# Four transposes of layer 3 go behind the next unit's first score in TensorE's queue

## The chip, the cores and the metric

One core of one Trainium2 chip runs the whole program in one launch. The metric is the device time in microseconds; the kernel before took 2738.4 us (median of 3 runs, 2736.6 to 2738.7). The profile shows one more execution, of 2738.3 us, with a span of 2737.0 us.

## The reference

Thirty-two sequences of 256 tokens with 256 features pass through four layers. Layer 0 is a conditioned MLP with a norm over the whole sequence, layer 1 is attention with 16 heads, an additive bias and a mask, and an MLP, layer 2 is a stencil over the 256 x 256 grid, layer 3 is causal attention with 16 heads and an MLP:

```
h  = layernorm(x, gamma1, beta1)
attn = softmax(causal(h Wq @ (h Wk)^T / 4)) @ (h Wv)
x1 = x + attn @ Wo + bo
h2 = layernorm(x1, gamma2, beta2)              # m4 (statistics), m4_norm, t4, t4_out
ff = gelu(h2 @ W1 + b1) @ W2 + b2              # w3, w3_out, w3_gelu, w4
x2 = x1 + ff
return x + gate * (x2 - x)
```

All of it is computed. The change touches only when the transposes of `h2` (before gamma2 and beta2) stand in TensorE's queue.

## The kernel before

The program is software-pipelined over a clock of ticks. A sequence b starts every 64 ticks; its layer 3 starts 160 ticks later than its layer 1. Each attention layer is cut into 8 units of two heads, one unit every 4 ticks, so layer 1 of a sequence and layer 3 of another take turns. Between the units' pieces stand the dense pieces of the layers (projections, MLPs, stencil, norms). The table `P` gives each piece its tick within its sequence or unit; `OWN` overrides it for the first two and the last two sequences. Each engine walks through the ticks and issues the pieces that are due, in a fixed order within a tick; nothing else sets the order. Engines wait for each other by semaphores, and each queue is in order: what stands behind a waiting instruction waits too.

On TensorE a tick issues first the attention pieces (score0, score1, flip0, flip1, pv0, pv1), then the dense ones; t4 and w3 are the last but one and two of the list. In the middle sequences the ticks 50 to 57 of layer 3 of sequence b hold, on TensorE: 50 score0 of unit 5 of layer 1 of sequence b + 3, 51 the flips of unit 3, 52 score1 of unit 5 and the pv pieces of unit 2, 53 t4, 54 score0 of unit 6, 55 the flips of unit 4 and w3 step 0, 56 score1 of unit 6 and pv of unit 3, 57 w3 step 1. Ticks 59 and 61 have w3 steps 2 and 3.

The pieces that the prediction follows:

- score0 (L1191): one matmul of the stacked queries Qs and keys Ks, 96 rows deep, into PSUM bank bS[0]. It waits for the stack (d_st) and for VectorE to have read the bank's previous score (v_bias, L786).
- The stack: for every second unit SP issues nine DMAs, three of Qs (L407) and six of Ks (L411), from SBUF to SBUF, into one of two buffers. SP's queue also has the bias loads BT (L396), which wait for VectorE's bias piece of four units earlier, and the loads of x and the mask.
- flip0, flip1 (L1199): four transposes each of the probabilities PB, after ScalarE's exp (L990). ScalarE copies them out as PH (L996).
- m4_norm (ScalarE, L1005): writes the normalised rows TC. t4 (TensorE, `turn`, L1163): four transposes of TC into bank bT_. t4_out (ScalarE, L1011): TN from that bank, with gamma2 and beta2. In ScalarE's queue: flip copies of unit 3, m4_norm, exp1 of unit 4, t4_out, exp0 of unit 5, flip copies of unit 4, w3_out step 0.
- w3 step g (TensorE, `widen`, L1171, eight matmuls of TN into bank bT_), w3_out step g (ScalarE, L1011, BB from the bank). One bank serves all four steps, so step g + 1 waits for w3_out of step g.

Of the kernel before, what the change touches and what calls it, by code (L numbers as in the profile page):

```python
# [42 lines left out]
def begin(layer, b):  # L43
# [32 lines left out]
}  # L76

LATE = {
# [44 lines left out]
        "s_b": 88, "s_r": 88, "s_rp": 90, "s_re": 95, "s_ha": 95, "s_w": 96, "s_ab": 97, "s_row": 98, "s_mm": 100,  # L123
# [3 lines left out]
    },  # L127
    1: {
        "score0_1": 1, "score1_1": 3, "bias0_1": 3, "exp0_1": 6, "flip0_1": 11, "flip1_1": 11, "high0_1": 12,
# [1311 lines left out]
```

## Time and profile before

| | us |
|---|---|
| median of 3 runs | 2738.4 |
| profiled execution, time | 2738.3 |
| its span | 2737.0 |
| TensorE matmul busy | 2599.0 |
| ScalarE busy | 2338.8 |
| VectorE busy | 2221.9 |
| GpSimd busy | 1674.0 |

A row of the time line gives the start, the length, the engine (PE is TensorE's matmuls, PEld its weight loads, DVE VectorE, ACT ScalarE, SPq SyncE's queue of DMA issues), the line, the operation, output and inputs by the program's names, the shape, how many instructions are merged (x4), and in brackets how long the engine sat idle before and what ended that. A matmul's length is its latency; the next one may start before it ends.

### The profile page before, as it was taken

Reading aid. Unit: us, or ns where it says so; the run is one execution under the profiler, and the core shown is the slowest. Engines: PE = TensorE matmul, PEld = TensorE weight load, DVE = VectorE, ACT = ScalarE, POOL = GpSimd, SP = SyncE. Lnnn points to the kernel's source line nnn. Section 1 sums busy time; section 2 is a strip of 40 time slices with the busy share of each in tenths; the row PEclk is TensorE's granted clock in tenths of the full one; section 3 lists DMA queues with packets and bytes.
Section 4 is the critical chain, followed back from the end, with each engine's and each line's share of the span. In section 5 each row is a group of like instructions: output and inputs, shape, how many; then the busy total and the mean of one; then the engine's idle time right before and its main releaser. Section 6 shows DMA issues by size and latency. Waiting matters only on the chain.

```text
span 2737.0 us, 62626 instructions
## 1 busy us (share of the span) xinstructions
PE 2599.0 (95%) x20072; PEld 2214.0 (81%) x20072; DVE 2221.9 (81%) x7925; ACT 2338.8 (85%) x5285; POOL 1674.0 (61%) x1742
## 2 busy tenths in 40 slices
PE   8888999999999999999999999999999999999987
PEld 7766888888888888888888888888888888888776
DVE  5668888888888888888888888888888888888753
ACT  1567899999999999998999989999998998999865
POOL 2666666766667675666666566666666666765431
PEclk8988999999999999999999999999999999999999
DMA  6433343333333333333333333343333333333211
GB/s 230 130 96 102 91 118 108 116 102 113 96 103 115 109 114 103 110 98 101 114 112 112 103 108 101 98 119 108 113 97 114 101 100 116 109 105 102 63 31 29
DMA packets 176549, 287.96 MB, mean 105 GB/s; under 512 B 45856, under 2 KB 99104, under 8 KB 175840
## 3 DMA queue, kind: packets, MB, share of 16 engines
q1 hardware_dynamic: 176224, 283.97, 35.2%
q8 instruction: 162, 2.65, 0.4%
q14 instruction: 163, 1.34, 0.2%
HBM read 174.64 MB, written 8.45 MB: 67 GB/s over the span
## 4 chain that ended last, share of the span: by engine, by line
PE 71%; ACT 13%; issue 4%; SPq 4%; DVE 3%; POOL 2%; DMA 2%; ACTq 0%; DVEq 0%; POOLq 0%
PE bank L1171 15%; PE bank L1178 14%; PE bank L1199 10%; PE bank L1156 9%; PE bank L1148 8%; PE bank L1191 5%; ACT PB L990 3%; PE bank L1163 3%; SPq L411 2%; ACT PH L996 2%; PE bank L1306 2%; ACT BB L1011 2%; PE bank L1217 2%; PE bank L1218 2%; ACT AA L1011 2%
## 5 line engine op out<-in xcount | busy, mean ns | idle before, releaser
L990 ACT ACTIVATE PB<-PB,mx 128x256 f32<-128x256 f32 (+1 forms) x2048 | 834.6, 475 | 6.0 <-DVE mx L786 5.2
L794 DVE TENSOR_TENSOR PO<-bank,PH 128x384 f16<-128x384 f32 (+1 forms) x1024 | 589.4, 616 | 247.5 <-ACT PH L996 244.4
L497 POOL TENSOR_TENSOR BT<-BT,MN 128x1024 f32<-128x1024 f32 x256 | 545.9, 2137 | 174.2 <-DMA BT<-in_bias 173.4
L996 ACT ACTIVATE PH<-bank 128x384 f16<-128x384 f32 (+1 forms) x1024 | 499.0, 538 | 127.7 <-PE bank L1199 127.2
L1191 PE MATMUL bank<-Ks,Qs 96*128 96x512 f32 (+1 forms) x1024 | 519.1, 510 | 19.5 <-DMA Ks<-KU 11.9
L1199 PE MATMUL bank<-ident,PB 128*128 128x128 f32 x3584 | 484.8, 275 | 8.5 <-ACT PB L990 4.5
L1199 PEld LDWEIGHTS bank<-ident,PB 128*128 128x128 f32 x3584 | 421.2, 142 | 46.8 <-ACT PB L990 12.3
L786 DVE CUSTOM_DVE_ANT_0 PB<-bank,BT 128x256 f32<-128x256 f32 x1024 | 386.7, 416 | 37.6 <-PE bank L1191 36.2
L786 DVE CUSTOM_DVE_ANT_0 PB<-bank,caus 128x128 f32<-128x128 f32 (+1 forms) x1024 | 321.0, 351 | 22.9 <-PE bank L1191 22.5
L1217 PEld LDWEIGHTS bank<-VP,PH 128*128 128x128 f16 x3584 | 204.0, 96 | 119.2 <-issue 93.5
L1171 PE MATMUL bank<-TN,Wf 128*128 128x256 f32 x1024 | 253.9, 391 | 16.6 <-ACT BB L1011 11.4
L1171 PE MATMUL bank<-MB,Wf 128*128 128x256 f32 x1024 | 251.9, 389 | 14.2 <-ACT AA L1011 13.0
L1217 PE MATMUL bank<-VP,PH 128*128 128x49 bf16 x3584 | 257.5, 186 | 7.8 <-DVE CX L807 2.7
L1218 PE MATMUL bank<-VP,PO 128*128 128x49 bf16 x3584 | 249.7, 184 | 0.0
L1178 PE MATMUL bank<-Wf,BB 128*128 128x256 f32 x1024 | 244.8, 384 | 0.7 <-ACT BB L1000 0.7
L1178 PE MATMUL bank<-Wf,AA 128*128 128x256 f32 x1024 | 239.3, 381 | 1.6 <-ACT AA L1076 1.6
L1191 PEld LDWEIGHTS bank<-Ks,Qs 96*128 96x128 f32 x1024 | 195.1, 191 | 41.2 <-DMA Ks<-KU 16.0
L1171 PEld LDWEIGHTS bank<-TN,Wf 128*128 128x128 f32 x1024 | 184.9, 190 | 51.5 <-ACT BB L1011 21.0
L1171 PEld LDWEIGHTS bank<-MB,Wf 128*128 128x128 f32 x1024 | 184.2, 190 | 45.7 <-ACT AA L1011 24.0
L1178 PEld LDWEIGHTS bank<-Wf,AA 128*128 128x128 f32 x1024 | 189.4, 190 | 27.0 <-issue 2.1
L1218 PEld LDWEIGHTS bank<-VP,PO 128*128 128x128 f16 x3584 | 207.9, 97 | 0.7
L1178 PEld LDWEIGHTS bank<-Wf,BB 128*128 128x128 f32 x1024 | 185.2, 190 | 22.2 <-issue 1.0
(225 smaller groups left out, 5208.8 us busy)
## 6 DMA issues: line engine op xcount, KB each, us to landing
BT<-in_bias SPq DMA_DIRECT2D x256, 512.0 KB, 3.9
Qs<-QH SPq DMA_DIRECT2D x512, 64.0 KB, 2.4
Ks<-KH SPq DMA_DIRECT2D x1024, 32.0 KB, 2.0
Qs<-QU SPq DMA_DIRECT2D x256, 64.0 KB, 2.5
Ks<-KU SPq DMA_DIRECT2D x512, 32.0 KB, 2.0
XT<-in_xT SPq DMA_DIRECT2D x32, 256.0 KB, 2.9
X<-in_x SPq DMA_DIRECT2D x32, 256.0 KB, 2.9
AB<-ada_rows SPq DMA_DIRECT2D x32, 256.0 KB, 3.6
```

Of the source, the lines that this page charges most:

```text
L497: G.op.tensor_tensor(v2(BT[k % 4]), v2(BT[k % 4]), MN[:, :].unsqueeze(1).broadcast_to([128, 2, 512]), ALU.add).then_inc(g_bt, 1)
L786: V.op.tensor_tensor_reduce(PB[(2 * D + q) % 6][:, h * 256:h * 256 + w], bS[q][:, h * w:h * w + w], plus, -1.0, 3.0e38, ALU.add, ALU.min, ...
L794: V.op.tensor_tensor(PO[i][:, 0:w], bP[h][:, 0:w], PH[i][:, 0:w], ALU.subtract).then_inc(v_low, 1)
L990: S.op.activation(o, o, ACT.Exp, scale=-1.0, bias=mx[u.layer][:, c:c + 1]).then_inc(a_exp, 1)
L996: S.op.activation(PH[i][:, 0:w], bP[h][:, 0:w], ACT.Copy).then_inc(a_high, 1)
L1156: last = T.op.matmul(half(ps, m), x[:, k * 256 + m * 128:k * 256 + m * 128 + 128], Wf[:, a + k * 256:a + k * 256 + 256], start=(k == 0), s ...
L1171: last = T.op.matmul(half(ps, f), Wf[:, c:c + 128], half(x, d), start=(d == 0), stop=(d == 1))
L1178: last = T.op.matmul(half(ps, q), x[:, f * 256 + q * 128:f * 256 + q * 128 + 128], Wf[:, c:c + 256], start=(g == 0 and f == 0 and q == 0), ...
L1191: T.op.matmul(bS[q][:, 0:2 * w].rearrange("p (h k) -> p h k", h=2), Qs[i][0:96, et * 256 + q * 128:et * 256 + q * 128 + 128], k2[:, :, 0:w ...
L1199: last = T.op.transpose(bP[h][:, c * 128:c * 128 + 128], PB[(2 * u.D + q) % 6][:, h * 256 + k * 128:h * 256 + k * 128 + 128], ident[:, :])
L1217: T.op.matmul(bV[:, o:o + 49], PH[i][:, c * 128:c * 128 + 128], vv, start=(n == 0), stop=False)
L1218: last = T.op.matmul(bV[:, o:o + 49], PO[i][:, c * 128:c * 128 + 128], vv, start=False, stop=(n == len(ks) - 1))
```

## The change

t4 goes from tick 53 to tick 54 in the general table. For the first sequence it already was at 54 by an entry of its own, which goes. The last two sequences have their own entries (153 and 578), which stay. So 29 of the 32 sequences have t4 one tick later. Within tick 54 the attention pieces come first.

```
 P = {
...
-    "t4": 53, "t4_out": 54, "w3": 55, "w3_out": 57, "w3_gelu": 67, "w4": 69, "out": 75, "st_out": 77,
+    "t4": 54, "t4_out": 54, "w3": 55, "w3_out": 57, "w3_gelu": 67, "w4": 69, "out": 75, "st_out": 77,
...
 OWN = { ... 0: {
-        "v3_sub": 0, "v3_mid": 4, "c3": 44, "m4": 47, "m4_rstd": 47, "t4": 54, "w3_gelu": 66, "out": 76, "st_out": 84,
+        "v3_sub": 0, "v3_mid": 4, "c3": 44, "m4": 47, "m4_rstd": 47, "w3_gelu": 66, "out": 76, "st_out": 84,
```

## Rows read from the trace of the kernel before

**Rows 1.** The page's part 1: busy time of each engine.
```profile
PE 2599.0 (95%) x20072; PEld 2214.0 (81%) x20072; DVE 2221.9 (81%) x7925; ACT 2338.8 (85%) x5285; POOL 1674.0 (61%) x1742
```

**Rows 2.** The table of waits: who waited for whom, us, times, longest.
```profile
PE bank L1163 <- ACT TC L1005: 24.2, 28, 1.6
...
PEld bank L1171 <- ACT TN L1011: 7.8, 22, 1.4
...
SPq L396 <- DVE mx L786: 368.5, 155, 8.1
```

**Rows 3.** The time line around the transposes of b = 9.
```profile
1025.98 0.42 DVE L786 CUSTOM_DVE_ANT_0 PB<-bank,BT 128x256 f32<-128x256 f32 x1
1025.99 1.09 ACT L1005 ACTIVATE TC<-Y,smt 128x256 f32<-128x256 f32 x2
...
1026.97 0.90 ACT L990 ACTIVATE PB<-PB,mx 128x256 f32<-128x256 f32 x2
...
1027.13 0.66 PE L1163 MATMUL bank<-ident,TC 128*128 128x128 f32 x4 [0.78 <-ACT TC L1005]
...
1027.54 0.48 PE L1191 MATMUL bank<-Ks,Qs 96*128 96x512 f32 x1
...
1027.83 1.02 ACT L1011 ACTIVATE TN<-bank,cols 128x256 f32<-128x256 f32 x2
1027.86 1.04 PE L1199 MATMUL bank<-ident,PB 128*128 128x128 f32 x8
...
1028.90 1.59 PEld L1171 LDWEIGHTS bank<-TN,Wf 128*128 128x128 f32 x8 [0.24 <-ACT TN L1011]
...
1030.93 0.84 ACT L1011 ACTIVATE BB<-bank,cols 128x256 f32<-128x256 f32 x2 [0.32 <-PE bank L1171]
...
1031.82 0.19 PEld L1171 LDWEIGHTS bank<-TN,Wf 128*128 128x128 f32 x1 [0.17 <-ACT BB L1011]
```

**Rows 4.** SP's time line, b = 9: the first and last issues of unit 6's stack.
```profile
1019.77 0.57 SPq L407 DMA_DIRECT2D Qs<-QH  x1
...
1024.25 1.23 SPq L411 DMA_DIRECT2D Ks<-KU  x2
```

**Rows 5.** The tile Ks, DMAs issued from 1024.0 to 1025.5.
```profile
DMA to landing us min/median/max: 2.0/2.0/2.0
```

**Rows 6.** SP's and TensorE's time lines, b = 15.
```profile
1502.30 1.67 SPq L407 DMA_DIRECT2D Qs<-QH  x1
...
1506.62 1.23 SPq L411 DMA_DIRECT2D Ks<-KU  x2
...
1508.42 0.66 PE L1163 MATMUL bank<-ident,TC 128*128 128x128 f32 x4 [0.78 <-ACT TC L1005]
...
1509.31 0.50 PE L1191 MATMUL bank<-Ks,Qs 96*128 96x512 f32 x1 [0.24 <-DMA Ks<-KU]
...
1510.41 1.17 PEld L1171 LDWEIGHTS bank<-TN,Wf 128*128 128x128 f32 x6
```

**Rows 7.** TensorE's time line at b = 10, 12 (two rows), 13 and 16.
```profile
1107.07 0.66 PE L1163 MATMUL bank<-ident,TC 128*128 128x128 f32 x4 [0.79 <-ACT TC L1005]
...
1266.99 0.66 PE L1163 MATMUL bank<-ident,TC 128*128 128x128 f32 x4 [0.78 <-ACT TC L1005]
1269.01 0.51 PE L1191 MATMUL bank<-Ks,Qs 96*128 96x512 f32 x1 [1.36 <-DMA Ks<-KU]
...
1348.51 0.66 PE L1163 MATMUL bank<-ident,TC 128*128 128x128 f32 x4 [0.69 <-ACT TC L1005]
...
1588.61 0.66 PE L1163 MATMUL bank<-ident,TC 128*128 128x128 f32 x4 [0.70 <-ACT TC L1005]
```

**Rows 8.** The tile Ks, b = 23, DMAs issued from 2146.6 to 2147.3.
```profile
DMA to landing us min/median/max: 2.4/2.5/2.7
```

**Rows 9.** Stretches of 6 us: length, busy time by engine, granted clock, DMA share.
```profile
1268.00:1274.00 6.00, 4.92 (x40) 4.23 (x41) 4.13 (x16) 4.43 (x11) 2.01 (x4) 1.00 0.29 71
...
2312.00:2318.00 6.00, 5.93 (x40) 5.10 (x39) 4.01 (x16) 3.91 (x10) 2.10 (x4) 0.77 0.35 89
```

## The prediction

> **What bounds the kernel now.** I read the page's first part, then the table of waits, then the time line around one of the moved groups, then SP's time line ahead of it.
>
> TensorE is busy 95% of the span, with ScalarE behind it [rows 1]. So a TensorE stall can be worth its length, if nothing else is late right behind it. The table of waits names the stall that this change is about: the first transpose of the normalised rows TC waits for ScalarE 28 times, 24.2 us in all [rows 2], about 0.86 us each, nearly always in the middle 28 sequences (b = 1 to 28). It is 0.9% of the time, and the most that filling it could return.
>
> The time line of b = 9 shows what stands around the stall [rows 3]. ScalarE ends the normalisation m4_norm at 1027.08 (1025.99 + 1.09) and the transposes start at 1027.13. Behind them stand the score (1027.54), the eight flip transposes (1027.86), and w3.0, the first matmuls of layer 3's feed-forward. In the same stretch ScalarE does m4_norm, exp1, t4_out, exp0 and the flip copies without a gap. The reader is to see the third wait: w3.0's weight load sits idle for 0.24 us until t4_out (ACT L1011, 1027.83 + 1.02) is done. The same wait stands 22 times in the table, 7.8 us [rows 2]. What ends last here is therefore m4_norm, t4, t4_out, w3.0, and not TensorE's queue.
>
> **The change, part by part.** Twenty-nine sequences (b = 1 to 29) get t4 one tick later; b = 0, 30 and 31 keep their order. No instruction is added or removed and no DMA moves. In tick 54 the attention pieces are issued first, so TensorE's order becomes score0 of unit 6, four transposes, eight flips, w3.0. Only the score and the transposes change places.
>
> What the stall takes up. The score can't start before its operands: its PSUM bank is free at 1026.40, when DVE has read the half before [rows 3], and its stack must have landed. SP issues the nine stack DMAs from 1019.77 on; the last starts at 1024.25 + 1.23 - 0.59 = 1024.89 [rows 4] and lands 2.0 us later [rows 5], at 1026.89. With 0.04 us for the semaphore (b = 15: landed 1507.26 + 2.0 = 1509.26, score 1509.31 [rows 6]) the score would start at 1026.93, not 1027.54. So 0.61 us of it is gained for the score.
>
> What the gain is worth. The score occupies the queue for 0.32 us (1027.54 to 1027.86, rows 3), so the transposes come at 1027.25 instead of 1027.13. The eight flips take 1.04 us, which is seven spacings of 0.11 and one matmul of 0.27; four transposes whose first load is hidden by the score take 3 x 0.11 + 0.27 = 0.60 (0.66 when it is not). Then 0.04 to t4_out, 1.02 for it, 0.05 to w3.0's load: w3.0 starts 1.71 us after the first transpose, at 1028.96. Before it was 1028.90. The flips would be through 0.2 us earlier, but w3.0 is what follows them, and it waits longer. The stall filled with 0.32 us of score comes back as 0.3 us more of wait at w3.0: gain nothing, cost 0.06.
>
> Where it costs. In b = 12 to 25 the stack is late, because one of its DMA issues is long: in b = 15 the third takes 1.67 us instead of 0.59, and the last DMA lands 0.84 us after the point at which the transposes began (1508.42) [rows 6]. Before, this wait (0.24 us of it seen) lay behind the transposes, so ScalarE did t4_out under it. After, the transposes wait with it: score 1509.31, transposes 1509.64, w3.0 1509.64 + 1.71 = 1511.35 instead of 1510.41. That is +0.94. What is queued behind the waiting score is t4, and for it wait t4_out, exp0, the flip copies on ScalarE and w3.0.
>
> The same sum over all of them, with L the landing less the transposes' start: the extra is L + 0.31 where that is positive, less what w3.0 already was late. I read it in each of the 28 periods from the same two rows, SP's last Ks issue and the first transpose; b = 9 [rows 3 to 5] stands for the fourteen periods with a stack in time or nearly so, b = 15 [rows 6] for the fourteen of b = 12 to 25. b = 1, 2, 4, 5, 26, 28: 0. b = 3, 7, 9, 10, 11, 18, 27: 0.05 to 0.11, together 0.56. b = 6, 8, 17: 0.25, 0.42, 0.34. b = 13, 14, 19: 0.68, 0.52, 0.52. b = 20, 23: 0.80, 0.77. b = 12, 15, 16, 21, 22, 24: 0.93 each, 5.6. b = 25: 0.1, since there w3.0 is late already. Sum 0.56 + 1.01 + 1.72 + 1.57 + 5.6 + 0.1 = 10.6 us. For b = 29 the order changes too, but exp holds t4_out there: 0.
>
> Is it kept until the end? The trace has delays of this size at this very place. From b = 9 to b = 10 the transposes are 79.94 us apart (1027.13, 1107.07). From b = 15 to 16 it is 80.19, with a wait of 0.24 at the score; from b = 12 to 13 it is 81.52, with a wait of 1.36 [rows 6, 7]. The delay is passed on whole. The reason is in rows 3: w3_out.0 waits 0.32 us for w3.0 on ScalarE and w3.1 waits 0.17 us for w3_out.0, one PSUM bank between them, so a late w3.0 moves all. Nor does SP run ahead and absorb it: it spends 368 us waiting for DVE before the bias loads [rows 2], each period anew. I take all 10.6 as kept; the bounds are 0 kept (see below) and 28 x 0.94 = 26 if every stack were as late as that of b = 15. I take the value read per period, as long issues fall at the same DMA of neighbouring sequences.
>
> The Trainium skill, "DMA: Bandwidth & Descriptors", section "Anatomy of one DMA — SWDGE (gpsimd) path", which is about DMAs that GpSimd issues, gives a nearly constant fixed cost of about 2.0 us to landing. Most stacks agree [rows 5]; in b = 22 to 25 the last transfers took up to 2.7 to 3.5 us (b = 23: 2.4 to 2.7 [rows 8]). With the constant the late stacks of these four would be in time and the sum would be about 8 us instead of 10.6. The rows decide.
>
> The profiled execution took 2738.3 us (span 2737.0 and 1.3 around it), the median is 2738.4. 2738.3 + 10.6 = 2748.9; I say 2749, 0.4% slower.
>
> **The rivals.**
> 1. The stall is filled and w3.0 doesn't give it back. Then each of 28 periods gains the score's 0.32 us: 9.0 us, 2729. For it speaks the table of waits, which shows the stall and an occupied TensorE. Against it, w3.0's 0.24 us wait in 22 periods: there at most a queue that is already early gets earlier. It needs ScalarE to reach t4_out earlier, and exp1 (1026.97 + 0.90) stands in front of it either way.
> 2. The delays are absorbed. Then 0 to 4 us, 2738 to 2742, no change that can be told. It needs waits of TensorE on something that doesn't move with it. Those that there are, for ScalarE (0.17 at w3.1), are for work that TensorE itself released. Or the long DMA issues fall elsewhere in a changed run.
> 3. The clock falls. TensorE's mean granted clock is 0.77 in 6 us of b = 25, right behind a stall and a late stack [rows 9], so a part of them ran at 1.2 instead of 2.4 GHz: 0.23 x 6 = 1.4 us of full-speed work lost. After the change the late periods have their idle time in one piece (b = 15: 1.67 us, from 1507.64 to 1509.31) and some 0.9 us more of it ahead of w3.0. If six of the fourteen late periods lose 1.4 us: 2749 + 8.4 = 2757. Against it: b = 12 had 0.78 + 1.36 us of idle time [rows 7] and its next 6 us are at 1.00 [rows 9].
> 4. The order doesn't change as said: excluded but for b = 0, 30 and 31, from the table of ticks (before: t4 53, score0 54).
>
> **How the numbers follow.** My forecast has 0.65, rival 1 has 0.07, rival 2 has 0.20, rival 3 has 0.08. What a measurement can tell from no change is 0.2%, 5.5 us; the forecast's 10.6 is twice that. Its own range is 2744 (half kept) to 2754 (half as much again; the bound is 26). The range for 8 in 10 goes from 2738 to 2757: it leaves out the gain and the worse half of rival 3. Faster 0.07, same 0.20, slower 0.73.
>
> **What the trace after would show.** The stall before the transposes of TC goes from the table, or shrinks, and scores waiting for the stack's DMA appear in its place, in b = 12 to 25 above all; the wait of w3.0 for TN rises from 0.24 to about 0.5 in early periods and 0.9 in late ones; early periods stay at 79.95 us apart and late ones grow by 0.3 to 0.9 us. I am wrong if early periods shrink to 79.6 (then w3.0 wasn't the end of the chain), if w3.0 starts late and the period doesn't grow (absorbed), or if the late stacks stop being late.

## The result, and the profile after

The kernel after takes 2751.1 us (median of 6 runs), the kernel before 2737.2 us in the same session: ratio 1.0053, 95% interval 1.0039 to 1.0068, so 11 to 19 us slower. The forecast was 2749 with a range of 2738 to 2757. The profiled execution took 2752.2 us with a span of 2750.9, 13.9 more than before.

The page's part 1 hardly moves (compare [rows 1]); TensorE is as busy as before in a span that is longer:

```profile
PE 2604.5 (95%) x20072; PEld 2219.8 (81%) x20072; DVE 2221.9 (81%) x7925; ACT 2339.7 (85%) x5285; POOL 1674.3 (61%) x1742
```

The table of waits (who waited for whom, us, times, longest) tells more. The row of the stall, 24.2 us at the transposes [rows 2], is gone altogether. The scores' wait for the stack's DMA went from 11.9 us in 13 waits to 35.8 in 34, and w3.0's wait for TN doubled from 7.8 in 22 to 15.2 in 28. What the stall gave up stands in these two rows, 31 us more in them against 24 less.

```profile
PE bank L1191 <- DMA Ks<-KU: 35.8, 34, 3.6
...
PEld bank L1171 <- ACT TN L1011: 15.2, 28, 1.4
...
SPq L396 <- DVE mx L786: 366.0, 143, 8.1
```

The time line of b = 9, one of the early periods (against [rows 3]): m4_norm ends at 1025.13, the score starts when its stack has landed, 0.16 us before that, and the transposes 0.18 us after it, where they had started after 0.05. w3.0 starts 1.89 us after m4_norm's end; it was 1.82. Its weight load now waits 0.48 us instead of 0.24.

```profile
1024.04 1.09 ACT L1005 ACTIVATE TC<-Y,smt 128x256 f32<-128x256 f32 x2
1024.97 0.50 PE L1191 MATMUL bank<-Ks,Qs 96*128 96x512 f32 x1 [0.58 <-DMA Ks<-KU]
1025.31 0.60 PE L1163 MATMUL bank<-ident,TC 128*128 128x128 f32 x4
1025.75 1.04 PE L1199 MATMUL bank<-ident,PB 128*128 128x128 f32 x8
1025.95 1.02 ACT L1011 ACTIVATE TN<-bank,cols 128x256 f32<-128x256 f32 x2
1027.02 1.59 PEld L1171 LDWEIGHTS bank<-TN,Wf 128*128 128x128 f32 x8 [0.48 <-ACT TN L1011]
```

The time line of b = 15, a late one (against [rows 6]): the score waits 1.15 us for its stack, the transposes are held behind it until 0.76 us after m4_norm's end (1509.85), and now ScalarE itself stands idle, 0.60 us, in front of t4_out. That wait did not exist before. w3.0 starts 2.47 us after m4_norm's end, before it was 2.05.

```profile
1508.76 1.09 ACT L1005 ACTIVATE TC<-Y,smt 128x256 f32<-128x256 f32 x2
1510.27 0.50 PE L1191 MATMUL bank<-Ks,Qs 96*128 96x512 f32 x1 [1.15 <-DMA Ks<-KU]
1510.61 0.60 PE L1163 MATMUL bank<-ident,TC 128*128 128x128 f32 x4
1511.25 1.02 ACT L1011 ACTIVATE TN<-bank,cols 128x256 f32<-128x256 f32 x2 [0.60 <-PE bank L1163]
1512.32 1.59 PEld L1171 LDWEIGHTS bank<-TN,Wf 128*128 128x128 f32 x8 [0.47 <-ACT TN L1011]
```

I split each span at the end of m4_norm of b = 1 and of b = 28 (start plus length of its row in the time line):

| profile | before b = 1 | b = 1 to 28 | behind b = 28 | m4_norm to w3.0, summed over 28 |
|---|---|---|---|---|
| before | 387.0 | 2165.4 | 184.6 | 54.5 |
| after | 384.4 | 2176.8 | 189.6 | 65.9 |

In the middle, 11.4 us are lost, and 11.4 are found in the 28 stretches from m4_norm's end to w3.0 (0.1 of it in the last one, which lies just behind the middle); the stretches between them, from w3.0 to the next m4_norm, agree within 0.2 us in sum. Ahead of b = 1, 2.6 us are won and behind b = 28, 5.0 lost; the first experiments show whether these belong to the change.

### The profile page after: what moved, and what is told of

Its sections match the earlier page's. It is cut to its first block, busy times and chain, and to the rows that moved or that the text cites. A ratio compares the mean times of both kernels' runs of the same rounds, so it can differ in the third digit from the quotient of the medians.

```text
span 2750.9 us, 62626 instructions
## 1 busy us (share of the span) xinstructions
PE 2604.5 (95%) x20072; PEld 2219.8 (81%) x20072; DVE 2221.9 (81%) x7925; ACT 2339.7 (85%) x5285; POOL 1674.3 (61%) x1742
## 4 chain that ended last, share of the span: by engine, by line
PE 73%; ACT 11%; SPq 5%; issue 4%; DVE 4%; DMA 2%; POOL 1%; ACTq 0%; DVEq 0%; POOLq 0%
PE bank L1178 16%; PE bank L1171 15%; PE bank L1199 10%; PE bank L1156 9%; PE bank L1148 9%; PE bank L1191 5%; SPq L411 3%; PE bank L1163 3%; ACT PB L990 2%; PE bank L1306 2%; ACT BB L1011 2%; PE bank L1217 2%; DMA Ks<-KU 2%; SPq L407 2%; ACT PH L996 2%
## 5 line engine op out<-in xcount | busy, mean ns | idle before, releaser
L1191 PE MATMUL bank<-Ks,Qs 96*128 96x512 f32 (+1 forms) x1024 | 518.4, 510 | 44.4 <-DMA Ks<-KU 35.8
L1171 PE MATMUL bank<-TN,Wf 128*128 128x256 f32 x1024 | 255.7, 393 | 22.4 <-ACT BB L1011 11.4
```

Source lines behind the costliest of these rows:

```text
L1171: last = T.op.matmul(half(ps, f), Wf[:, c:c + 128], half(x, d), start=(d == 0), stop=(d == 1))
L1191: T.op.matmul(bS[q][:, 0:2 * w].rearrange("p (h k) -> p h k", h=2), Qs[i][0:96, et * 256 + q * 128:et * 256 + q * 128 + 128], k2[:, :, 0:w ...
```

## The experiments

Ratios are to the kernel before, run on the same chip, with their 95% intervals in brackets. Behind each time stand 5 to 12 runs, unless said otherwise.

**The same kernel again, and the one group outside the pattern.** The first is `before` unchanged (one run); the second:

```
 OWN = {
+    -3: {"t4": 54},          # b = 29 only; P["t4"] stays 53
```

> The kernel before, profiled once more. Between the last group of b = 28 and the end the kernel after lost 5 us more than the sum over the groups explains, and before b = 1 it had won 2.6 us. If that is chance of where TensorE's clock falls in the first and last hundred microseconds, this profile shows shifts of 1 to 3 us against the first profile of the same kernel there, and none between b = 2 and b = 24 apart from waits for late stacks. If it belongs to the change, the two profiles agree within 0.3 us everywhere.

> Only the group of b = 29, the one outside the pattern, goes behind the score; all others stay where they were. Theory (exp1 holds t4_out there, so it costs nothing): 0 us, ratio 1.000 within 0.001. Rival (the 5 us lost behind b = 28 come from this one group): 2 to 5 us slower, ratio 1.001 to 1.002.

Measured: the same kernel took 2741.7 us in its one run, with 387.9, 2165.2 and 187.3 us in the three parts. `e_only29`: 2736.9 us, ratio 0.9996 (0.9985 to 1.0006), parts 383.7, 2164.2 and 188.4. The first part runs from 383.7 to 387.9 and the last from 184.6 to 188.4 in these three; `e_early_b` and `e_mask_b` below, which also keep the old order, have 191.0 and 189.6 in the last. So the 2.6 us won and 5.0 lost there by the kernel after are of the size of chance. The group of b = 29 costs nothing that can be measured: the interval ends at 1.0006, below the 1.001 of the rival. The middle is steady: 2165.4, 2165.2, 2164.2. Against these the kernel after, with 2176.8, loses 11.4 to 12.6 us. The second half of my expectation was too strict: single late stacks also differ between two profiles of one kernel (below), and the clock fell once more in the middle.

**An early stack, in both orders.** The stack of unit 6 of layer 1 (from sequence 4 on, which is the one that stands beside the 28 groups) goes one tick earlier in SP's queue, ahead of the bias load that waits for VectorE; with `t4` at 53 it is `e_early_b`, with 54 `e_early_a`.

```
-            due[piece].setdefault(starts[u.D][0] + place(piece, u.b, NB, f"_{u.layer}"), []).append(u)
+            due[piece].setdefault(starts[u.D][0] + place(piece, u.b, NB, f"_{u.layer}")
+                + (-1 if piece == "stack" and (u.layer, u.n) == (1, 6) and 4 <= u.b else 0), []).append(u)
```

> The kernel before, with the stack of unit 6 of layer 1 issued one tick earlier on SP, ahead of the bias load that waits for DVE, so that it lands some 2.4 us earlier in all 28 sequences. Theory: only the waits of the score behind the transposes go, 2.8 us in all: 2734 us, ratio 0.999; the stall before the transposes stays at 0.8 us. A cost of its own (the bias load comes up to 4 us later) would show as POOL waiting longer for BT.

> The kernel after, with the same early stack. Theory (the loss is t4 held behind a score that waits for its stack, and w3.0 gives back whatever the filled stall gains): the loss is gone and there is no gain, the same time as the early stack with the order of before, 2734 to 2736 us, ratio 0.998 to 1.000; w3.0 waits 0.5 us for TN. Rival 1 (the stall would have been worth filling, the late stacks hid it): 9 us faster than the early stack with the order of before, 2725. Rival 2 (the new order costs by itself, whenever the stack lands): still 10 to 14 us slower, 2745 to 2750.

Measured: `e_early_b` 2738.5 us, ratio 1.0002 (0.9991 to 1.0014); `e_early_a` 2735.5 us, ratio 0.9998 (0.9986 to 1.0009). The parts b = 1 to 28 are 2161.5 and 2161.9 us, 3.9 and 3.5 less than before. The stack now lands 1.1 to 3.7 us before m4_norm's end in every one of the 28 sequences. So the new order costs nothing once the stack is in time, which fells rival 2 of these expectations, and gains nothing either, which fells its rival 1. Time lines of b = 9, first `e_early_b`, then `e_early_a`; the last row of each is m4_norm of b = 10:

```profile
1026.11 1.09 ACT L1005 ACTIVATE TC<-Y,smt 128x256 f32<-128x256 f32 x2
...
1027.25 0.66 PE L1163 MATMUL bank<-ident,TC 128*128 128x128 f32 x4 [0.78 <-ACT TC L1005]
...
1027.66 0.48 PE L1191 MATMUL bank<-Ks,Qs 96*128 96x512 f32 x1
...
1029.02 1.59 PEld L1171 LDWEIGHTS bank<-TN,Wf 128*128 128x128 f32 x8 [0.24 <-ACT TN L1011]
...
1106.04 1.09 ACT L1005 ACTIVATE TC<-Y,smt 128x256 f32<-128x256 f32 x2
```

```profile
1023.57 1.09 ACT L1005 ACTIVATE TC<-Y,smt 128x256 f32<-128x256 f32 x2
1024.14 0.47 PE L1191 MATMUL bank<-Ks,Qs 96*128 96x512 f32 x1 [0.20 <-DVE mx L786]
...
1024.71 0.66 PE L1163 MATMUL bank<-ident,TC 128*128 128x128 f32 x4
...
1026.47 1.59 PEld L1171 LDWEIGHTS bank<-TN,Wf 128*128 128x128 f32 x8 [0.47 <-ACT TN L1011]
...
1103.52 1.09 ACT L1005 ACTIVATE TC<-Y,smt 128x256 f32<-128x256 f32 x2
```

From m4_norm's end to w3.0 it is 1.82 and 1.81 us, and from this m4_norm to that of b = 10 it is 79.93 and 79.95. In the second the score sits in the stall, and w3.0's wait has grown from 0.24 to 0.47: this is the give-back, seen alone. The early stack gives the kernel before no measurable gain, though its middle part is shorter by 3.9 us.

**A late stack, in both orders.** The same edit with `6` instead of `-1`, which puts the stack behind the mask load (0.69 us from its issue to the next).

> The kernel before, with the stack of unit 6 of layer 1 moved behind the mask load on SP, so that it lands 0.69 us later in the 28 sequences. Theory: the score behind the transposes has some 0.6 us of slack, so the fourteen early periods pay nothing and the late ones 0.1 to 0.69: about 7 us slower, 2744 us, ratio 1.0025. Rival (late landings cost nothing as such): 0.

> The kernel after, with the same stack behind the mask load. Theory (with the transposes behind the score every microsecond of landing goes through t4 and t4_out to w3.0): 0.69 us in each of 28 sequences, 19 us slower than the kernel after, 2770 us, ratio to before 1.012; 26 us behind the same edit in the order of before. Rival (the order costs a fixed amount): the distance between the two orders stays at 14 us, 2758.

Measured: `e_mask_b` 2745.0 us, ratio 1.0028 (1.0015 to 1.0040), so 4 to 11 us slower; `e_mask_a` 2769.1 us, ratio 1.0114 (1.0091 to 1.0136), 25 to 37 us. The distance between the orders is 24 us, where 26 were expected and a fixed cost would have left 14. In the middle part it is 28.0 us (2166.8 and 2194.8). That both come so near to 26 is in part luck: two errors offset each other. In the early periods the stack lands 0.5 us later and not 0.69 (b = 9: from 0.2 us before m4_norm's end to 0.3 behind it). And the granted clock of TensorE falls six times in the middle of `e_mask_a` and once in that of `e_mask_b`, which is some 5 us of the 28; without it the orders are some 23 us apart, still far from a fixed 14. At b = 9 the stack lands 0.3 us after m4_norm's end in both. With the old order that is hidden, w3.0 comes after 1.82 us as ever; with the new one after 2.40. The time line of `e_mask_a` at b = 9 has the whole chain: the score waits 1.06 us, ScalarE 0.53 in front of t4_out, w3.0 0.48.

```profile
1032.50 1.09 ACT L1005 ACTIVATE TC<-Y,smt 128x256 f32<-128x256 f32 x2
...
1033.93 0.51 PE L1191 MATMUL bank<-Ks,Qs 96*128 96x512 f32 x1 [1.06 <-DMA Ks<-KU]
...
1034.91 1.02 ACT L1011 ACTIVATE TN<-bank,cols 128x256 f32<-128x256 f32 x2 [0.53 <-PE bank L1163]
1035.98 1.59 PEld L1171 LDWEIGHTS bank<-TN,Wf 128*128 128x128 f32 x8 [0.48 <-ACT TN L1011]
```

**w3 one tick later, in both orders.** `e_w3_b` is before with w3 at 56; `e_w3_a` is after with w3 at 56 and the early stack. This takes the wait for TN out of w3.0's way. The two differ in two things, the order and the early stack, so their times alone don't show what the order is worth.

```
-    "t4": 53, "t4_out": 54, "w3": 55, "w3_out": 57,       (54 for t4 in e_w3_a)
+    "t4": 53, "t4_out": 54, "w3": 56, "w3_out": 57,
```

> The kernel before, with the four w3 steps one tick later, so that w3.0 stands behind score1 and the pv pieces and not right behind the flips. Theory: it no longer waits for TN; TensorE's order is otherwise the same and the stall before the transposes stays: 0 to 6 us faster (up to the 0.24 us of w3.0's wait in 28 sequences), or slower if w3_out then holds the flip copies on ScalarE back. Serves as the partner of the next.

> The kernel after with the early stack and w3 one tick later: both that swallow the gain are out of the way. Theory (the stall is worth filling only if what follows does not wait for TN): the score's 0.32 us in 28 sequences comes through, 9 us faster than the same w3 edit in the order of before; against the kernel before 5 to 12 us faster, ratio 0.996. Rival (TensorE's queue isn't the bound even then, ScalarE's is: m4_norm, exp1, t4_out, exp0 without a gap): the same as its partner within 3 us.

Measured: `e_w3_b` 2759.2 us, ratio 1.0085 (1.0069 to 1.0101); `e_w3_a` 2752.9 us, ratio 1.0057 (1.0041 to 1.0074). Both lose, against what I expected of them by themselves. Their distance is 6.3 us, but it holds the early stack too, and the two intervals overlap; the periods with the stack in time in both kernels separate the two. Time lines of b = 9, first `e_w3_b`, then `e_w3_a`; the last row of each is m4_norm of b = 10:

```profile
1032.09 1.09 ACT L1005 ACTIVATE TC<-Y,smt 128x256 f32<-128x256 f32 x2
...
1033.23 0.66 PE L1163 MATMUL bank<-ident,TC 128*128 128x128 f32 x4 [0.78 <-ACT TC L1005]
...
1035.47 1.59 PEld L1171 LDWEIGHTS bank<-TN,Wf 128*128 128x128 f32 x8
...
1038.39 0.73 PEld L1171 LDWEIGHTS bank<-TN,Wf 128*128 128x128 f32 x4 [0.79 <-ACT BB L1011]
...
1112.81 1.09 ACT L1005 ACTIVATE TC<-Y,smt 128x256 f32<-128x256 f32 x2
```

```profile
1036.73 1.09 ACT L1005 ACTIVATE TC<-Y,smt 128x256 f32<-128x256 f32 x2
...
1037.87 0.66 PE L1163 MATMUL bank<-ident,TC 128*128 128x128 f32 x4
...
1039.88 1.59 PEld L1171 LDWEIGHTS bank<-TN,Wf 128*128 128x128 f32 x8
...
1042.80 0.73 PEld L1171 LDWEIGHTS bank<-TN,Wf 128*128 128x128 f32 x4 [0.79 <-ACT BB L1011]
...
1117.22 1.08 ACT L1005 ACTIVATE TC<-Y,smt 128x256 f32<-128x256 f32 x2
```

w3.0 has no wait in either, and comes 2.29 us after m4_norm's end in the first and 2.06 in the second. At b = 9 the stack is in time in both, and from this m4_norm to that of b = 10 it is 80.72 and 80.49 us; the other periods with a stack in time have the same, 80.71 and 80.46 in most. So here the filled stall is worth about 0.25 us a sequence, 0.23 of it ahead of w3.0, where with w3 at 55 it was worth nothing (79.93 and 79.95). So the wait for TN at w3.0 was what swallowed the gain. Over 28 sequences this is an estimate of some 7 us; that the times are 6.3 apart is partly chance, since the late stacks cost `e_w3_b` 3.8 us more and other small delays cost `e_w3_a` about as much. What both lose against the kernel before: w3.0 comes 0.47 and 0.24 us later, and from w3.0 to the next m4_norm it takes 0.3 us longer (78.42 against 78.13 in most periods). The last row but one of each shows where: w3.1 now waits 0.79 us for w3_out.0 (0.17 before, [rows 3]), since one PSUM bank ties each w3 step to the copy of the last.

**The stall taken away on ScalarE.** m4_norm goes ahead of the flip copies: `"m4_norm": 52` to `51`, t4 at 53.

> The kernel before, with m4_norm one tick earlier on ScalarE, ahead of the flip copies of unit 3: the normalised rows are there when TensorE comes to the transposes, which stay ahead of the score. The stall of 0.8 us before the transposes is thus gone without any reordering on TensorE. Theory (what follows, t4_out behind exp1 and w3.0 behind t4_out, ends at the same time, since ScalarE has the same work in front of t4_out): no gain, 2737 us, ratio 0.998 to 1.002, and w3.0 waits up to 1 us for TN instead. Rival (the stall was 24 us of lost TensorE time): 10 to 20 us faster, 2717 to 2727.

Measured: 2754.6 us, ratio 1.0056 (1.0040 to 1.0072). There is no gain, so the rival is out, but the theory forecast no loss either, and that was wrong. Time line of b = 9, with m4_norm of b = 10 in the last row:

```profile
1034.25 1.10 ACT L1005 ACTIVATE TC<-Y,smt 128x256 f32<-128x256 f32 x2 [0.27 <-POOL smt L464]
...
1035.40 0.66 PE L1163 MATMUL bank<-ident,TC 128*128 128x128 f32 x4
...
1036.76 0.92 PEld L1199 LDWEIGHTS bank<-ident,PB 128*128 128x128 f32 x8 [0.52 <-ACT PB L990]
...
1037.00 1.01 ACT L1011 ACTIVATE TN<-bank,cols 128x256 f32<-128x256 f32 x2
...
1038.06 1.59 PEld L1171 LDWEIGHTS bank<-TN,Wf 128*128 128x128 f32 x8 [0.38 <-ACT TN L1011]
...
1114.24 1.09 ACT L1005 ACTIVATE TC<-Y,smt 128x256 f32<-128x256 f32 x2 [0.29 <-POOL smt L464]
```

The stall before the transposes is gone here and the score follows, yet TensorE waits 0.52 us for exp1 at the flips and 0.38 for TN at w3.0: the idle time has moved once more. I had not seen that m4_norm, moved forward, waits 0.27 us for GpSimd's factor, which ScalarE had spent on the copies. This wait by itself costs nothing: from this m4_norm to the next it is 79.99 us, 79.94 before, as t4_out still stands behind exp1. The middle part is 12.8 us longer, and 11.1 of that stand in twelve periods, b = 1 to 4, 12 and 21 to 27. All four falls of the clock in the middle lie in them (one before), and so do most of the long waits of m4_norm for GpSimd, 0.7 to 1.8 us. Which of these costs how much I did not follow.

**The whole chain forward.** Early stack, m4_norm 51, t4_out 53 (ahead of exp1), w3 54 (ahead of the flips), w3_out 55.

> The kernel before, with the whole chain moved forward: early stack, m4_norm ahead of the flip copies, t4_out ahead of exp1, w3.0 ahead of the flips of unit 4, w3_out two ticks earlier. Theory (the chain m4_norm, t4, t4_out, w3.0 and the w3 steps with one bank is the bound of this stretch): w3.0 starts about 0.5 us earlier, up to 14 us faster, 2723 to 2737, if the flips, now behind w3.0, don't make DVE's subtraction and the pv pieces late. Rival (the attention units' own loop, exp, flips, copies, subtraction, pv, is just as tight): it loses about as much as the flips come later, 1 to 2 us per sequence, 2765 to 2795.

Measured: 2802.9 us, ratio 1.0226 (1.0206 to 1.0246): 63 us slower, beyond the end of the rival's range (2795). Time line around b = 9:

```profile
1054.24 1.59 PEld L1171 LDWEIGHTS bank<-TN,Wf 128*128 128x128 f32 x8 [1.30 <-ACT TN L1011]
...
1057.64 1.29 DVE L794 TENSOR_TENSOR PO<-bank,PH 128x512 f16<-128x512 f32 x2 [1.01 <-ACT PH L996]
...
1059.61 0.84 ACT L1011 ACTIVATE BB<-bank,cols 128x256 f32<-128x256 f32 x2 [1.52 <-PE bank L1171]
```

With t4_out in front of the exp and w3.0 in front of the flips, TensorE's weight loads stand idle 1.30 us in front of w3.0, where it was 0.24, and the attention units' own loop pays for it (DVE waits 1.01 us for the copies, ScalarE 1.52 for w3.1). The middle part is 56.7 us longer; the stretches from m4_norm to w3.0 are as long as before in sum, so all of it is lost behind w3.0. Five edits stand together here, so which of them costs most is not shown. No version that I tried beats the kernel before.

## Why the prediction was right

The mechanism held, and the sum was near.

- **Gain nothing.** Shown by the early stack in both orders (1.0002 and 0.9998; 79.93 and 79.95 us from b = 9 to 10) and by the w3 pair, where the same fill is worth 0.25 us a sequence as soon as w3.0 does not wait for TN. In the kernel after, the early periods are 80.02 us and not shorter: the forecast cost of 0.06, and not a gain of 0.3.
- **Cost by landing.** I had w3.0 at 2.08 us after the landing of the stack (0.04 + 0.33 + 1.71). In the kernel after it is 2.10 in every late period without a fall of the clock (b = 15: landed at 0.38 after m4_norm's end, w3.0 at 2.47; b = 12: 1.85 and 3.94; b = 8: 0.25 and 2.35). The late stack in both orders shows the same from outside: 24 us apart, 26 expected.
- **Size.** 10.6 us forecast; 11.4 lost in the middle, nearly all of it between m4_norm's end and w3.0. Falls of the clock make up 0.3 to 0.4 of that, so the landings cost about 11. The clock also fell at b = 14 and b = 21, where it had not before; each of these periods is about 1.2 us longer than 2.10 + 78.13 us from the landing gives (1.17 and 1.19). Of these 2.4 us, 2.0 stand behind w3.0, where the other small delays of the kernel before were larger by about as much; that these cancel to within 0.2 us is luck. Single periods came out otherwise (b = 15: 0.94 forecast, 0.42 measured; b = 14: 0.52 and 1.26, of which 0.4 is the clock), because the length of the long DMA issue changes from run to run. The sum carries over: the same working on the profiles of `before_again` and `e_only29` gives 10.3 and 11.9 us.
- **One reason was too simple.** I put all late stacks of b = 12 to 25 down to a long DMA issue. In b = 22 to 25 it is mainly the last transfer, which took 2.7 to 3.5 us to land in the kernel before and again in the kernel after, and not 2.0; and the stacks of b = 17 and 18 were hardly late before. The sum, read period by period from the landings, doesn't depend on it.
- **Kept until the end.** From w3.0 to the next m4_norm it is 78.11 to 78.14 us in most periods of both kernels, also behind a late w3.0 (b = 16: w3.0 at 2.06 us before and 3.04 after, and 78.14 behind it in both); the delays of w3.0 were passed on whole.
- **Rival 3, the falling clock,** was a small part of the result. Three stretches of the kernel after, against one of 0.77 before [rows 9] (columns: stretch, length, busy time of each engine, granted clock, DMA):

```profile
1426.50:1432.50 6.00, 4.59 (x33) 4.15 (x34) 4.86 (x18) 4.91 (x11) 4.46 (x3) 0.72 0.31 74
1994.00:2000.00 6.00, 5.31 (x23) 4.46 (x24) 4.33 (x14) 3.62 (x9) 2.54 (x3) 0.72 0.29 71
2318.00:2324.00 6.00, 4.63 (x34) 4.19 (x30) 4.53 (x18) 4.58 (x10) 4.55 (x4) 0.72 0.29 70
```

  The third has its counterpart before, in the 0.77 of the same sequence, b = 25. I priced a fall at 1.4 us, it was 1.2. In `e_mask_a`, with more idle time at this place, there are six. But the unchanged kernel had a second one too in its repeat (2068 to 2074 us, also 0.72), and `e_only29` had none in the middle, so one profile of each does not prove that the change brings them.
- **One sign was misread.** I expected w3.0 to wait 0.9 us in the late periods. It waits 0.47; the idle time stands at the score instead (1.15 us at b = 15), since the transposes and the flips that follow a late score fill the same 1.2 us whenever it comes.

## What to carry to other kernels

Before filling a stall on the busiest engine, look at the next wait on the same engine: if it ends on a chain that runs through the stalled instruction (here m4_norm, t4, t4_out, w3.0), the fill comes back there as wait. Then ask what the instruction that is moved forward waits for itself: it puts its own lateness, which used to be hidden behind the other work, in front of that chain. A stall that sits in front of a late input is also cover for it.

## What the runs showed of the hardware that I had not expected

SP's long DMA issues are tied to the place in its program. In SP's time line, some issues of Qs and Ks take 0.9 to 2.8 us instead of 0.6. Counted over SP's DMAs, with the first as number 1, the numbers 125, 1502, 1588 and 1604 are long in both profiles of the kernel before and in that of the kernel after; 173 and 1050 are long in both of the kernel before. Of the 108 long ones (0.85 us or more) in the profile of before, 56 have the same number in its repeat and 90 the same or one beside it, where places drawn by chance would give some 13. A sequence has 86 DMAs. In the stacks of unit 6 the long ones of b = 13 to 21 are number 1378, 1463, 1550, 1636, 1725, 1811, 1897, 1983 and 2069 in the profile of before, 85 to 89 apart, so one falls into each of these stacks, as it does in the repeat and in the kernel after; none falls into those of b = 1 to 11. Their length changes: at b = 12 the profile of before had 2.80 us at the second issue, its repeat had 0.59:

```profile
1260.24 2.80 SPq L407 DMA_DIRECT2D Qs<-QU  x1
```

```profile
1261.15 0.59 SPq L407 DMA_DIRECT2D Qs<-QU  x1
```

What SP does in them the profile does not tell.

The transfer itself varied too: a last Ks DMA of 32 KB took 2.0 us to land at b = 9 [rows 5] and 2.4 to 2.7 at b = 23 [rows 8]. The Trainium skill, "DMA: Bandwidth & Descriptors", section "Anatomy of one DMA — SWDGE (gpsimd) path", which is about DMAs that GpSimd issues, gives a DMA a nearly constant cost and a part that grows with its size. By that, DMAs of one size would take one time. These, which SP issues, agree at b = 9 and not at b = 23, and what varied most here, the issue of 2.80 or 0.59 us at one place, came before the transfer.
